# Second attention begun between the last units of the first, in one merged order

## The reference

```python
xn = _layernorm(x)                              # x: 8 batches x 256 tokens x 256
x = x + delta_rule_attention(xn) + experts0(xn) # 16 heads, L0
xn = _layernorm(x)
x = x + ttt_attention(xn) + experts1(xn)        # L1
# ttt_attention, for each chunk of 64 tokens, 2 heads:
qkv = silu(xn @ W_qkv); q, k = normed by column
lr = softplus(xn @ W_lr + b_lr + BASE_LR_INV)   # 6 rates a token
gate = k @ w0; hb = k @ w2; dhidden = v @ w1.T
g = gradients of w0, w1, w2, weighted by lr
w = w + newtonschulz5(g)                        # 2 rounds, for each of the three weights
w = w / norm(w) * norm(initial w)
out = silu(q @ w0) * (q @ w2) @ w1              # with the new weights
# experts1 chooses 2 of 6 experts for each batch by the mean of xn over its tokens
```

## Time and profile before

| what | us |
|---|---|
| median of 3 runs (1847.51 to 1849.9) | 1848.72 |
| the profiled execution | 1841.73 |
| its span, first to last instruction | 1839.9 |

### The profile page before, as it was taken

One profiled execution on the slowest core, in us unless ns is written; L12 is line 12 of the kernel. 1 busy time (PEld: TensorE's weight loads), 2 busy tenths in 40 slices (PEclk: granted clock), 3 DMA queues, 4 the chain that ended last, 5 costly groups with the idle time before them and its releaser, 6 DMA issues.

```text
span 1839.9 us, 43452 instructions
## 1 busy us (share of the span) xinstructions
PE 1719.3 (93%) x14326; PEld 1270.0 (69%) x14326; DVE 1442.2 (78%) x3395; ACT 1207.0 (66%) x2921; POOL 1082.1 (59%) x1144
## 2 busy tenths in 40 slices
PE   5999899999999999999999999999977788888878
PEld 4467567777777777777777777777755466666656
DVE  4322489999999999999999999999945688888853
ACT  1124467777777777777777777777744478778853
POOL 1510057777777777776666656666652377778841
PEclk8999999999999999999999999999976799999999
DMA  9423110110110110100000001000000000000032
GB/s 310 147 82 114 55 30 21 36 30 26 32 34 26 29 34 20 37 23 20 29 14 26 23 17 29 23 17 23 14 1 1 1 1 1 2 1 2 2 86 88
DMA packets 58668, 69.22 MB, mean 38 GB/s; under 512 B 10607, under 2 KB 47231, under 8 KB 58367
## 3 DMA queue, kind: packets, MB, share of 16 engines
q1 hardware_dynamic: 55511, 59.46, 10.9%
q0 software_dynamic: 3072, 8.65, 1.4%
HBM read 51.00 MB, written 17.10 MB: 37 GB/s over the span
## 4 chain that ended last, share of the span: by engine, by line
PE 84%; DVE 7%; ACT 5%; issue 1%; POOL 1%; SPq 1%; DMA 0%; DVEq 0%; ACTq 0%; POOLq 0%
PE banks L689 19%; PE banks L830 6%; PE banks L786 4%; PE banks L805 3%; PE banks L717 3%; PE banks L709 3%; PE banks L701 3%; PE banks L814 3%; PE banks L760 3%; PE banks L642 3%; PE banks L899 2%; PE banks L746 2%; PE banks L754 2%; PE banks L753 2%; PE banks L970 2%; PE banks L661 2%
## 5 line engine op out<-in xcount | busy, mean ns | idle before, releaser
L689 PE MATMUL banks<-xnT,hw 128*128 128x512 f32 x768 | 412.7, 621 | 1.7 <-DVE cv L1824 1.7
L1865 DVE CAST_PREDICATED MM<-lmask,banks 128x512 bf16<-128x512 uint32 x384 | 273.0, 711 | 64.8 <-PE banks L754 42.9
L1348 ACT ACTIVATE T<-banks 128x256 bf16<-128x256 f32 x384 | 147.1, 383 | 226.9 <-PE banks L746 214.2
L1824 DVE SCALAR_TENSOR_TENSOR cv<-banks,hc,cv 128x510 f32<-128x510 f32 (+2 forms) x384 | 277.8, 737 | 4.8 <-ACT cv L1298 4.1
L2368 POOL TENSOR_TENSOR X<-X,yrow 128x512 f32<-128x512 f32 x128 | 161.5, 1283 | 72.7 <-ACT yrow L1380 72.7
L746 PEld LDWEIGHTS banks<-MM,Gb 128*128 128x128 bf16 x1536 | 92.0, 98 | 86.7 <-issue 49.6
L830 PE MATMUL banks<-ho,OT 128*128 128x256 f32 x512 | 143.2, 403 | 0.0
L754 PEld LDWEIGHTS banks<-MM,T 128*128 128x128 bf16 x1536 | 104.2, 98 | 55.7 <-issue 31.9
L1824 DVE SCALAR_TENSOR_TENSOR cv<-banks,hcv,cv 128x510 f32<-128x510 f32 (+2 forms) x192 | 141.2, 735 | 0.8 <-ACT cv L1298 0.7
L2334 POOL TENSOR_TENSOR kn<-nsum,half_pos 128x4 f32<-128x4 f32 x64 | 65.6, 1025 | 126.4 <-DVE nsum L1836 126.4
L754 PE MATMUL banks<-MM,T 128*128 128x64 bf16 x1536 | 136.5, 193 | 0.0
(11 more groups left out here) (321 smaller groups left out, 4918.0 us busy)
## 6 DMA issues: line engine op xcount, KB each, us to landing
MM<-in_eye SPq DMA_DIRECT2D x64, 256.0 KB, 2.6
slot_rows<-zeros SPq DMA_DIRECT2D x1, 5304.0 KB, 20.5
xs<-slot_rows SPq DMA_DIRECT2D x13, 408.0 KB, 3.9
slot_out<-ye SPq DMA_DIRECT2D x13, 384.0 KB, 2.7
hw<-in_hw SPq DMA_DIRECT2D x16, 256.0 KB, 3.5
wgu<-in_wgu SPq DMA_DIRECT2D x1, 2816.0 KB
w1c<-in_ew SPq DMA_DIRECT2D x16, 176.0 KB
X<-in_x SPq DMA_DIRECT2D x4, 512.0 KB, 5.7
```

Source lines behind the costliest of these rows:

```text
L689: ins = pe.matmul(PROJ[t][:], hw[:, kk, t, :], xnT[:, kk, u.b * BLK:(u.b + 1) * BLK], start=(kk == 0), stop=(kk == KD - 1))
L1348: act.activation(strips(T1[:].rearrange("p i t -> p (i t)"), LEVELS[lv], 0, 1), grams_bank(u)[:, 0:TILES * 64].rearrange("p (k e) -> p k e ...
L1824: dve.scalar_tensor_tensor(o, y, taps_of(t)[:, TAPS - 1 - i:TAPS - i], o, ALU.mult, ALU.add).then_inc(dve_conv, 1)
L1865: dve.copy_predicated(dst, m, ps).then_inc(dve_mm, 1)
```

## The change

The four draining periods, the stage between the attentions and the periods 0 to 2 of the second are written as one list of steps per engine, in which the units a61 to a63 and the pairs x0, x1 and x2 alternate. `pair_period` runs from n = 3. What goes with it:

- the norm of group g, its turns and its rate logits stand where unit a60 + g has left; the turned halves lie in other PSUM banks, and `second_turn` has other waits;
- the rates are made for each pair by itself: `rate_logits(p)` on PE, `rates_begin(p)` on DVE, `rate_powers(p)` on POOL (e to the power of minus the amount of the logit, 24 columns, where ACT had an exponential of 96), `rates_end(p)` on DVE (13 instructions on 24 columns, where there were 13 on 96);
- the initial weights come by DMA straight to each pair's place, six DMAs a pair; for pairs 0 and 1 ahead of the head loop, over the weights of the first experts, which are no longer needed, for pairs 2 and 3 behind the last unit's solve;
- the softmax of the expert gate keeps its exponential on ACT, right before `pair_period(3)`, with a table load on either side, and `choose_experts` stands behind period 4.

The core of the diff:

```diff
-        EARLY = 2
-
         def second_bank(g, kk):
 
-            return bank[2 * kk] if g < EARLY else bank[(3, 5, 7, 3)[2 * (g - EARLY) + kk]]
+            return bank[4] if g == 2 else bank[2 * g + kk]
+
+        def weights_loaded(p):
+
+            return t_wload, 6 * 16 * max(p + 1, 2)
...
+            def load_weights(p):
+
+                for b in range(2):
+                    sp.dma_start(wT[p][:, :, 2 * b:2 * b + 2, :], a["winit"][:, 0]).then_inc(t_wload, 16)
+                    for m in range(2):
+                        sp.dma_start(w02[p][:, 2 * b:2 * b + 2, m, :], a["winit"][:, 1, m]).then_inc(t_wload, 16)
+
+            for n in range(YBUF):
+                sp.wait_ge(e_stored[n], 16 * len(range(n, GROUPS, YBUF)))
+            load_weights(0)
+            load_weights(1)
             with sp.Fori(0, NH - 1) as h:
                 load_head(h + 1)
+            sp.wait_ge(pe_solve, 12 * UNITS)
+            load_weights(2)
+            sp.wait_ge(pe_y, 2 * UNITS)
+            sp.wait_ge(*weights_loaded(2))
+            load_weights(3)
...
+                if g == 0:
+                    pe.wait_ge(dve_conv, 9 * UNITS)
+                elif g == 1:
+                    pe.wait_ge(act_last, UNITS)
+                elif g == 2:
+                    pe.wait_ge(act_mean, UNITS - 1)
+                    if kk == 1:
+                        pe.wait_ge(ln_kept0, NBLK + 2 + g + 1)
+                else:
+                    pe.wait_ge(act_y, 2 * UNITS)
...
-            for j in range(NBLK):
-                period(NH, j)
-            for g in range(EARLY):
-                for kk in range(KD):
-                    second_turn(g, kk)
-            for p in range(EARLY):
-                rate_logits(p)
-            for g in range(EARLY, NBLK):
-                for kk in range(KD):
-                    second_turn(g, kk)
-            pe.wait_ge(t_const, 6 * 16)
-            pe.wait_ge(*t_half)
...
+            second_turn(0, 0)
+            second_turn(0, 1)
+            invert(a63, 8)
+            first_solve(a62, 1)
+            times_gram(a62, 1, 0)
+            invert(a63, 9)
+            rate_logits(0)
+            correct(a62, 1, 0)
+            invert(a63, 10)
+            project_qk(x0)
+            times_gram(a62, 1, 1)
+            invert(a63, 11)
+            project_v(x0)
+            correct(a62, 1, 1)
+            invert(a63, 12)
+            outputs(a62)
+            first_solve(a63, 0)
+            second_turn(1, 0)
+            times_gram(a63, 0, 0)
+            second_turn(1, 1)
+            rate_logits(1)
+            correct(a63, 0, 0)
+            sums(a62)
+            times_gram(a63, 0, 1)
+            project_out(a62, 0)
+            correct(a63, 0, 1)
+            project_out(a62, 1)
+            carry(a63)
+            turn_qk(x0)
+            first_solve(a63, 1)
+            turn_v(x0)
+            times_gram(a63, 1, 0)
+            gates(x0)
+            hidden_back(x0)
+            project_qk(x1)
+            correct(a63, 1, 0)
+            times_gram(a63, 1, 1)
+            correct(a63, 1, 1)
+            outputs(a63)
...
+            total(x0)
...
+            total(x1)
+            for n in range(3, STEPS):
...
+            act.wait_ge(*f_lg)
+            act.activation(lge[:], lg[:], ACT.Exp).then_inc(act_once, 1)
+            act.activation(table[:, 1:2], onw[:], ACT.Silu)
+            for n in range(3, STEPS):
...
-            step(dve.tensor_tensor(wisq[:], winit[:, 0], winit[:, 0], ALU.mult))
-            step(dve.tensor_reduce(wn6[:], wisq[:].rearrange("p m h d -> p (m h) d"), AX.X, ALU.add))
-            assert steps == START_NORM_STEPS
-            for p in range(NP):
-                for b in range(2):
-                    dve.tensor_copy(wT[p][:, 0:2, 2 * b:2 * b + 2, :], winit[:, 0, 0:2])
...
+            def rates_begin(p):
+
+                dve.wait_ge(*t_rlog[p])
+                step(dve.tensor_tensor(lrz, bank[2 * p + 1][:, 0:NCH * 6].rearrange("p (c e) -> p c e", c=NCH),
+                                       blr[:].unsqueeze(1).to_broadcast([P, NCH, 6]), ALU.add))
+                dve.scalar_tensor_tensor(lra, lrz, -1.0, lrz, ALU.mult, ALU.min).then_inc(t_rpow, 1)
+
+            def rates_end(p):
+
+                y = lr[:, :, p, :]
+                dve.wait_ge(t_rpow, 2 * p + 2)
+                step(dve.tensor_scalar(y, lra, 2.0, None, ALU.add))
+                step(dve.reciprocal(y, y))
+                step(dve.tensor_tensor(lrq, lra, y, ALU.mult))
+                step(dve.tensor_tensor(lrs, lrq, lrq, ALU.mult))
+                step(dve.tensor_scalar(y, lrs, 2.0 / (2 * LOG_TERMS - 1), None, ALU.mult))
+                for n in range(LOG_TERMS - 2, -1, -1):
+                    step(dve.scalar_tensor_tensor(y, y, 2.0 / (2 * n + 1), lrs if n else lrq, ALU.add, ALU.mult))
+                dve.scalar_tensor_tensor(y, lrz, 0.0, y, ALU.max, ALU.add).then_inc(t_rate, 1)
+                dve.wait_ge(t_rate, p + 1)
...
+            rates_begin(1)
+            residual(a63, 0, 1)
+            norm_qk(x0, 1)
+            refine(a63, 0, 1)
+            norm_qk(x0, 2)
+            second_rhs(a63)
+            second_rhs_half(a63)
+            rates_end(1)
+            residual(a63, 1, 0)
+            norm_stats(2, 1)
+            refine(a63, 1, 0)
...
-                if n == 2:
+                if n == 4:
...
+            def rate_powers(p):
+
+                pool.wait_ge(t_rpow, 2 * p + 1)
+                pool.tensor_tensor(lra, euler, lra, ALU.pow).then_inc(t_rpow, 1)
...
+            rhs_minus(a62, 1, 1)
+            gram_rest(a63)
+            rate_powers(0)
+            rhs_minus(a63, 0, 0)
+            add_squares(a62)
+            root_qk(x0)
+            rhs_minus(a63, 0, 1)
+            inverse_rms(a62)
+            rate_powers(1)
+            add_rows(a62, 0)
+            add_rows(a62, 1)
+            rhs_minus(a63, 1, 0)
```

479 lines of the change are left out of this document (352 added, 127 removed).

## The result

| | us | ratio to before |
|---|---|---|
| before, median of 5 runs (1842.77 to 1849.9) | 1847.51 | |
| after, median of 5 runs (1829.49 to 1835.77) | 1833.25 | 0.9929 [0.9913, 0.9944] |
| after, a second series, 7 runs (1829.63 to 1844.8) | 1839.16 | 0.9935 [0.991, 0.996] |
| forecast | 1823.0 | 0.986 |

The change makes the kernel faster, by 12 to 13 us by the two ratios, where 25.6 were forecast. (The medians differ by 14.3 us and, in the second series, beside a before of 1848.48, by 9.3.) The profiled execution of after took 1829.49 us with a span of 1827.7, against 1841.73 and 1839.9.

A forecast was written before the change was run, and what follows sets the result against it. No engine was the bound: engines wait for each other over 120.6 us, TensorE partly at 1.2 GHz. Legs of 87.9 us gain 32.7; - 5.5 - 2.2 + 3.6 - 3.0 leaves 25.6, so 1848.72 becomes 1823, range 1809 to 1841.

The forecast's parts named there:

- legs 1, 2 and 4: First drain period, then to the end of outputs(a62), and from outputs(a63) to total(x0): 18.3, 12.3 and 11.6 us.
- the four powers: GpSimd's powers of 24 columns for the rates: 4.4 us each, by a line through three widths.
- the table loads: ScalarE's gate exponential and two table loads right before period 3: 3.0 us, of which about 2.2 isn't covered.
- leg 3: From the end of outputs(a62) to the end of outputs(a63): 21.9 us, against 19.4 before.
- the 5.4, taken from a62: In a63's solve, from the first correction to the second solve: 5.4 us, after a62's 1350.21 to 1356.36.
- leg 5: From total(x0) to total(x1): 23.8 us against 21.8 before, and 3.0 more for a slower clock.
- S3: Period 3 of TensorE, total(x1) to total(x2): 22.7 us, a full 20.5 plus 2.2 for the table loads.
- choose_experts: Moved on VectorE from behind period 2 to behind period 4: a cost of 5.5 us, at least 2.9.
- The tail: The last stage, from total(x15) to the end: said to be not touched, no cost charged.
- The power's: Rival: GpSimd's power holds VectorE at four places, about 3.7 times paid; 1839 at 8.8 us; slower from 11.3 us, chance 0.05.
- The clock: Rival: legs 2 to 5 run at a clock of 0.7, 15 us longer less 3 charged: 1835; chance 0.18.
- nothing overlaps: Rival: units and pairs take turns in every queue, some 4 us remain: 1845; chance 0.07 shared with a dear power.

The follow-up runs named there:

- pow_cheap: After with GpSimd's power in the rates replaced by a multiplication by a constant, everything else in place; ratio to before 0.9911.
- rates1_moved: After with rates_end(1) moved behind sum_qk(x1) and norm_stats(2, 1) moved ahead of a63's residual on VectorE; ratio to before 0.9922.
- best2: best with rates_end(3) moved in period 3 from behind the scaling of x1's gradients to behind through_silu(x2); 1819.2 us, ratio to before 0.9855.
- choose_spread: After with choose_experts cut into six pieces of 4 instructions behind through_silu in periods 4 to 9; 1826.66 us, ratio to before 0.988.
- best: After with the edits of rates1_moved and choose_spread, leg 5 reordered, rates_end(3) in period 3, the gate's exponential earlier; 1816.57 us, ratio to before 0.9847.
- no_exp: After with the expert gate's exponential replaced by a square, so ScalarE needs no table load; 1830.54 us, timed once.
- fill_both: After with four unread TensorE matmuls added in the wait before total(x0) and four in the tail behind the first gelu; 1833.45 us, timed once.

## Why the prediction was right on the sign and twice too large

**Right.** The legs 1, 2 and 4 within 0.8 us; `outputs(a63)` 60 us after the drain's start, later than before as the text said, though by 13 us and not by 5; the four powers, 4.17 us for 4.4 taken from the line through three widths; the full period 20.54 us; the loads of weights, which nothing waits for; the table loads, 2.16 us of keep for 2.2. The rule of the Trainium skill's "ScalarE: Activation LUTs", section "What ACT_TABLE_LOAD costs", that the prediction weighed and left out would have put 2.8 us on top; no drain of that kind is in the rows of after either.

**The term that failed most: leg 3, 21.9 us for 28.9.** The leg falls into four pieces, which end where TensorE starts the first correction, the second solve, the correction of that solve, and where `outputs(a63)` ends:

| piece | predicted us | after | pow_cheap | rates1_moved |
|---|---|---|---|---|
| to the first correction | 5.2 | 6.0 | 5.0 | 6.0 |
| to the second solve | 5.4 | 8.9 | 6.7 | 8.9 |
| to its correction | 6.6 | 6.2 | 6.1 | 4.4 |
| to the end of `outputs(a63)` | 4.7 | 7.8 | 7.8 | 5.5 |

The piece that failed most is the 5.4, taken from a62: it holds the 3.1 us of slow matmuls and the wait of 1.30 us for the cast, and the prediction had charged the clock to leg 5 alone (3.0 us, where 1 to 2 are shown). A cheap first power shortens it by 2.2 us. The last piece had 1.92 us of norm in it and so 2.8 for everything else, which without the norm took 5.5. The step "The layout has the residual at 1383.0 and TensorE free for its correction at 1384.7, so TensorE's inserted work and GpSimd's power end almost together" failed as well: the residual came last, 1.57 us behind TensorE. It had reckoned 2.9 to 3.2 us for `rates_end`. That is right with no GpSimd addition beside it (2.9 twice in best2), but the two here took 4.0 and 5.8. That piece still isn't longer than forecast, because TensorE's inserted work had been laid out 2 us too long. Moving rates and norm away gave back 4.2 of the 7.0 us, in the last two pieces, and the cheap power 3.2, in the first two; the two were not tried together.

**S3: 22.7 us for 23.0, and 24.6 to 25.1 in five other profiles with ScalarE's order unchanged.** That the sum is near is luck, for two errors met. Without the loads S3 takes 19.3 us, not 20.5; and the loads cost 3.7 or more, not 2.2, since behind a wait of 1.34 us come slow gates too.

**choose_experts: 5.5 us for 6.8.** Its own place costs 6.6 by choose_spread. That it could be had for 0.1 us a period was not thought of: the prediction read the 3.1 us of VectorE's idle time per period as a bound on what one block costs, and not as room for pieces.

**The tail: nothing for 2 to 3.4 us.** "The last stage is not touched" is true of the text; its time differs all the same, by 1.4 us or more, in eleven of the twelve profiles of the changed order and its variants; in one of them (best) it is 87.1 again.

**The rivals.** The power's was mis-sized in its slope: the prediction had 0.93 us paid for each us of power, downwards it is 0.28. What a longer power would cost was not tried. The clock cost more in sum: 3.1 us in the second piece of leg 3, 1 to 2 in leg 5, 2.2 in S3. In leg 3 and S3 it rose where a wait was taken away, so there it followed the waits; but the same wait does not always bring it down, as best and best2 show. Nor does it go with the busy share alone, as the prediction read it: in the earlier trace rows TensorE is 84% busy in a stretch at 0.90 and 85% in one at 0.69. That nothing overlaps is out, with 23.9 us gained up to `total(x1)`. The sums: 25.6 less 5.8 for the five legs with their clock, 1.3 for `choose_experts`, 2.0 for the tail, 0.3 for S3 and the chance 3.8 at the front make 12.4, and the two spans differ by 12.2.

**Open.** Why the second `up` of the tail runs at 1.2 GHz in the changed order and at 2.4 GHz in before and in best. The wait ahead of it is 3.14 to 3.17 us in those three profiles (before twice, best) and 3.19 to 3.31 in the ten others that have it. No run changed it by itself, and filling it kept the clock but delayed the `up`.

## What to carry to other kernels

Work that is pushed into another stage's waits is paid in the order of the queue it joins: ask of each inserted block which instruction of the old chain stands behind it, and put it behind that one, even where the block's own input is long ready. A block of small instructions needs no place of its own if a period has a gap at a fixed point: in pieces it is nearly free. And price small VectorE instructions by rows with GpSimd busy beside them, if that is where they will run.

## What the runs showed of the chip

A small VectorE instruction (128 x 24, 0.18 us alone) that starts beside a GpSimd addition, product or mask lasts until that ends, up to 1.25 us, in each of the three forms tried, while a reciprocal keeps its 0.30. This has no exception in the twelve profiles of the changed order and its variants: 113 instructions of `rates_end` in these forms start so and end 0.03 to 0.08 us behind GpSimd's, and all 48 reciprocals take 0.30. GpSimd's power holds nothing up in this way: the 154 that start beside one take 0.17 to 0.19. The power takes 1.01, 2.46 and 4.17 us for 4, 12 and 24 columns, near one line (which gave 4.4 for the last) for exponents of 0.5 and for data. And behind waits of TensorE of 1.3 to 2.2 us in leg 3, leg 5 and S3 matmuls ran at 1.2 GHz; with the wait gone (`times_gram` in rates1_moved, the gates in no_exp) or filled (the turn in fill_both) they ran at 2.4. It is no rule: behind the same wait of 2.2 us the gates of x1 ran at 1.2 GHz in best and at 2.4 in best2.
